# Attention with rotary embedding and a gated mixture of experts on one core: projections of q and k one step earlier, layer norm's scaling on ScalarE, weight pieces stored in order of use

## What is computed

```
x = x + tanh(g_xattn) * xattn(layernorm(x), ctx, ctx, wq, wk, wv, wo)
x = x + tanh(g_ffn) * ffn(layernorm(x), ...)

layernorm(x) = (x - mean) / sqrt(var + 1e-5)
xattn: qh, kh = rope(q @ wq.T), rope(k @ wk.T);  vh = v @ wv.T
       scores = qh . kh * 64**-0.5, masked to j <= i and j >= i - 64
       out = softmax(scores) @ vh;  return out @ wo.T
ffn:   shared = sum over 2 of gelu(x @ up.T) @ down.T
       gate = softmax(x @ router_w.T), all but the 4 largest set to 0
       routed = sum over 16 of (gelu(x @ up.T) * gate) @ down.T
```

## Time and profile before

| | |
|---|---|
| median of the runs | 569.51 us |
| the profiled execution's own time | 570.26 us |
| its span in the profile | 568.4 us |
| mean granted TensorE clock | 0.976 |
| busy: PE, DVE, ACT, POOL | 525.7, 343.6, 292.7, 274.7 us |

### The profile page before, as it was taken

One profiled execution on the slowest core, in us unless ns is written; L12 is line 12 of the kernel. 1 busy time (PEld: TensorE's weight loads), 2 busy tenths in 40 slices (PEclk: granted clock), 3 DMA queues, 4 the chain that ended last, 5 costly groups with the idle time before them and its releaser, 6 DMA issues.

```text
span 568.4 us, 13047 instructions
## 1 busy us (share of the span) xinstructions
PE 525.7 (92%) x4914; PEld 463.4 (82%) x4914; DVE 343.6 (60%) x1075; ACT 292.7 (51%) x832; POOL 274.7 (48%) x187
## 2 busy tenths in 40 slices
PE   8869789999989999899899879999999999999997
PEld 5558678889878888788887767888989898899996
DVE  5946486565965756865577553756464646554444
ACT  3275555656466555557556675554335333533332
POOL 2898886687678668767967961620010001000000
PEclk9979899999989999989999989989999999999999
DMA  7622403110031011001202227400900090036000
GB/s 241 195 51 77 107 15 95 34 35 14 23 104 36 3 34 35 10 26 35 70 3 52 73 75 248 144 1 4 329 5 1 27 309 2 1 96 240 1 1 37
DMA packets 20173, 41.02 MB, mean 72 GB/s; under 512 B 2896, under 2 KB 3152, under 8 KB 20112
## 3 DMA queue, kind: packets, MB, share of 16 engines
q1 hardware_dynamic: 20112, 40.20, 22.6%
HBM read 30.62 MB, written 2.23 MB: 58 GB/s over the span
## 4 chain that ended last, share of the span: by engine, by line
PE 72%; DVE 13%; issue 6%; ACT 3%; POOL 3%; DMA 1%; POOLq 0%; SPq 0%; DVEq 0%; ACTq 0%
PE ring L802 48%; PE psS L802 8%; PE psO L1000 5%; PE psS L969 5%; PE psT L981 4%; DVE xn L618 3%; DVE arena L638 2%; DVE arena L635 1%; ACT prob L540 1%; DVE wl L705 1%; DVE oTl L692 1%; DVE prob L684 1%; DMA x<-in_x 1%; DVE stats L607 1%; PE psT L942 1%
## 5 line engine op out<-in xcount | busy, mean ns | idle before, releaser
L802 PE MATMUL ring<-xTh,wh 128*128 128x512 f32 x272 | 110.8, 407 | 2.9 <-DVE wl L705 1.3
L802 PE MATMUL ring<-xTh,wl 128*128 128x512 f32 x272 | 106.5, 392 | 0.0
L802 PE MATMUL ring<-xTl,wh 128*128 128x512 f32 x272 | 106.0, 390 | 0.0
L484 ACT ACTIVATE sneg<-ring 128x512 f32<-128x512 f32 x72 | 43.3, 601 | 108.8 <-PE ring L802 99.3
L802 PE MATMUL ring<-wh,oTh 128*128 128x256 f32 x272 | 79.9, 294 | 7.9 <-ACT arena L526 5.7
L684 DVE TENSOR_TENSOR prob<-sneg,arena 128x512 f32<-128x512 f32 x64 | 44.1, 690 | 68.5 <-ACT sneg L484 68.5
L400 POOL TENSOR_TENSOR arena<-arena,sin 128x1024 f32<-128x1024 f32 x29 | 69.7, 2403 | 29.6 <-DVE arena L635 29.6
L413 POOL TENSOR_TENSOR prob<-prob,rinv 128x512 f32<-128x512 f32 x64 | 66.9, 1045 | 31.6 <-DVE rinv L767 30.8
L802 PE MATMUL ring<-wh,oTl 128*128 128x256 f32 x272 | 78.5, 289 | 0.0
L802 PE MATMUL ring<-wl,oTh 128*128 128x256 f32 x272 | 78.3, 288 | 0.0
L408 POOL TENSOR_TENSOR arena<-arena 128x1024 f32<-128x1024 f32 x29 | 68.9, 2377 | 1.2
(11 more groups left out here) (116 smaller groups left out, 1229.2 us busy)
## 6 DMA issues: line engine op xcount, KB each, us to landing
arena<-gate_scratch SPq DMA_DIRECT2D x64, 256.0 KB, 6.5
raw<-in_e SPq DMA_DIRECT2D x18, 256.0 KB, 2.7
raw<-in_w SPq DMA_DIRECT2D x16, 256.0 KB, 3.4
arena<-arena SPq DMA_DIRECT2D x16, 256.0 KB, 3.1
arena<-arena SPq DMA_DIRECT2D x16, 192.0 KB, 3.4
craw<-in_ctx SPq DMA_DIRECT2D x4, 512.0 KB, 3.4
x<-in_x SPq DMA_DIRECT2D x4, 512.0 KB, 4.8
out<-x SPq DMA_DIRECT2D x8, 256.0 KB, 3.1
```

The costliest lines, as they stand in the source:

```text
L484: act.activation(act_g[:, n % 2, :], ring[0][:, n % 2, :], ACT.Gelu).then_inc(f_gelu, 1)
L802: last = pe.matmul(out, a, b, start=start and i == 0 and j == 0, stop=stop and i == n - 1 and j == 2, skip_group_check=check)
```

## The change

It moves jobs in the list of steps, and each engine follows:

- q of unit u + 2 is projected in step 3 of unit u, ahead of y (before: q of unit u + 1 in step 0). k of unit u + 1 is projected in step 0 instead of step 1; in the last unit of a batch it stays in step 1. v stays in step 2. The transposes of the next batch's `xn` move from step 2 to step 1 of the third unit.
- POOL turns and joins q in step 0 and k in the steps 1 and 2 (2 and 3 in the last unit of a batch), and divides ahead of turning.
- At the start k of unit 1 leaves the prologue for step 0, and q of unit 1 enters it.
- ACT writes `xn` as `rstd * x + shift`. POOL makes `shift` = -mean * rstd with two more small operations.
- Weight pieces are numbered by `ORDER`, in order of use, and made two a step in unit 0 and one a step in unit 1. Of the experts' pieces 4 are made before the expert phase instead of 8, besides the two shared ones.

```diff
+ORDER = [("k", 0), ("v", 0), ("q", 0), ("q", 1), ("k", 1), ("v", 1), ("y", 0), ("q", 2), ("k", 2), ("v", 2),
+         ("y", 1), ("q", 3), ("k", 3), ("v", 3), ("y", 2), ("y", 3)]
+PIECE_OF = {name: i for i, name in enumerate(ORDER)}
+PRELOADED = 4
...
         prologue = [("ctx", 0), ("w", 0), ("stat", 0), ("w", 1), ("norm", 0), ("w", 2), ("k", 0),
-                    ("v", 0), ("xT", 0), ("warm", 2), ("w", 3), ("w", 4), ("q", 0), ("w", 5), ("w", 6),
-                    ("k", 1), ("warm", 3)]
+                    ("v", 0), ("xT", 0), ("warm", 2), ("w", 3), ("q", 0), ("w", 4), ("q", 1), ("warm", 3)]
...
-            if k == 0 and u + 1 < UNITS:
-                jobs.append(("q", u + 1))
-            if k == 1 and 1 <= u and u + 1 < UNITS:
+            if k == (1 if g == GROUPS - 1 else 0) and u + 1 < UNITS:
                 jobs.append(("k", u + 1))
-            if (u, k) == (0, 1) or (k == 2 and 1 <= u and u + 1 < UNITS):
+            if k == (1 if u == 0 else 2) and u + 1 < UNITS:
                 jobs.append(("v", u + 1))
-            if k == 2 and g == 2 and b + 1 < B:
+            if (g, k) == (2, 1) and nextb:
                 jobs.append(("xT", b + 1))
+            if k == 3 and u + 2 < UNITS:
+                jobs.append(("q", u + 2))
             if k == 3 and u >= 1:
                 jobs.append(("y", u - 1))
...
-            if u < 2 and k >= 2:
-                jobs += [("w", 8 + 4 * u + 2 * (k - 2)), ("w", 9 + 4 * u + 2 * (k - 2))]
+            if u == 0:
+                jobs += [("w", 5 + 2 * k), ("w", 6 + 2 * k)]
+            if u == 1 and k < 3:
+                jobs.append(("w", 13 + k))
...
-            if UNITS - 2 <= u < UNITS:
-                jobs.append(("w", expert_piece(NS + 4 * (u - (UNITS - 2)) + k)))
+            if UNITS - 2 <= u < UNITS and k % 2:
+                jobs.append(("w", expert_piece(NS + 2 * (u - (UNITS - 2)) + k // 2)))
...
+                late = int(u % GROUPS == GROUPS - 1)
+                if k == 0 and u + 1 < UNITS:
+                    if c:
+                        divide(c - 1)
+                    turn(0, u + 1)
+                    join(0, u + 1)
+                elif 1 <= c <= CHUNKS:
+                    divide(c - 1)
                 if u + 1 < UNITS:
-                    if k == 1:
-                        turn(0, u + 1)
-                        join(0, u + 1)
-                    if k == 2 and u:
+                    if k == 1 + late:
                         turn(1, u + 1)
-                    if k == 3 and u:
+                    if k == 2 + late:
                         join(1, u + 1)
...
+            def normalise(j):
+                act.wait_ge(ln_rstd, j + 1)
+                if j:
+                    act.wait_ge(xT_pe, j)
+                for t in range(TT):
+                    last = act.activation(xn[:, t, :], x[:, j % B, t, :], ACT.Identity,
+                                          bias=shift[:, t:t + 1], scale=rstd[:, t:t + 1])
+                last.then_inc(ln_norm, 1)
```

More of the change, by code:

```diff
@@ L223, in build @@
         after = {n: [] for n in range(N + 2)}
-        for e in range(NS + 8, NE):
-            after[e - 8].append(("w", expert_piece(e)))
+        for e in range(NS + PRELOADED, NE):
+            after[e - PRELOADED].append(("w", expert_piece(e)))
         for b in range(B - 1):
@@ L396, in turn @@
             def turn(i, n):
[L397 to L402, removed]
+                part = swap[:, i, :, :]
+                pool.wait_ge(qk_swap[i], rotated(n))
+                link(pool.tensor_tensor(part, part, sin[:, :].unsqueeze(1).to_broadcast(part.shape),
+                                        ALU.mult))
             def join(i, n):
                 dst = (qT[:, n % 2, :, :], kT[:, n % 2, :, W:])[i]
[L406 to L409, removed]
+                pool.wait_ge(qk_mul[i], rotated(n))
+                pool.tensor_tensor(dst, dst, swap[:, i, :, :], ALU.add).then_inc(qk_rot[i], 1)
             def divide(c):
@@ L427, in do @@
                                        ALU.subtract).then_inc(c_lo, 1)
-                elif kind in "qk" and n < 1 + (kind == "k"):
+                elif (kind, n) in (("q", 0), ("k", 0)):
                     i = "qk".index(kind)
-                    if n == 0:
+                    if kind == "k":
                         pool.wait_ge(in_rope, 32)
[L432 to L436, removed]
-                                                sin[:, :].unsqueeze(1).to_broadcast(part.shape),
-                                                ALU.mult))
-                        pool.wait_ge(qk_mul[i], done)
-                        pool.tensor_tensor(dst[:, pairs, :], dst[:, pairs, :], part,
-                                           ALU.add).then_inc(qk_rot[i], 1)
+                    for pair in range(2):
+                        part = swap[:, i, pair, :]
+                        dst = (qT, kT)[i][:, 0, pair, W * i:W * i + L]
+                        pool.wait_ge(qk_swap[i], pair + 1)
+                        link(pool.tensor_tensor(part, part, sin[:, :], ALU.mult))
+                        pool.wait_ge(qk_mul[i], pair + 1)
+                        pool.tensor_tensor(dst, dst, part, ALU.add).then_inc(qk_rot[i], 1)
                 elif kind == "stat":
@@ L611, in statistics @@
                 last.then_inc(ln_stat, 1)
-            def normalise(j):
-                dve.wait_ge(ln_rstd, j + 1)
-                if j:
-                    dve.wait_ge(xT_pe, j)
-                for t in range(TT):
-                    last = dve.tensor_scalar(xn[:, t, :], x[:, j % B, t, :], mv[:, t, 0:1],
-                                             rstd[:, t:t + 1], ALU.subtract, ALU.mult)
-                last.then_inc(ln_norm, 1)
             def rotate(job):
@@ L1064 @@
     wo = a(L0_xattn_wo).reshape(D, GROUPS, 2, P).transpose(1, 3, 2, 0).reshape(GROUPS, P, PIECE)
-    w = np.stack([wk, wv, wq, wo], 1).reshape(WPIECES, P, PIECE)
+    by_kind = dict(k=wk, v=wv, q=wq, y=wo)
+    w = np.stack([by_kind[kind][g] for kind, g in ORDER])
     up = np.concatenate([a(L0_ffn_shared_up), a(L0_ffn_routed_up)]).reshape(NE, P, KC, P)
```

37 lines of the change are left out of this document (19 added, 18 removed).

## The result

| | before | after |
|---|---|---|
| median of the runs | 569.5 us | 574.5 us |
| profiled execution: its own time, span | 570.26, 568.4 us | 574.98, 573.2 us |
| mean granted clock | 0.976 | 0.984 |
| scores of unit 2 start at | 63.85 us | 72.64 us |
| unit 2 to unit 15 | 259.6 us | 247.8 us |

The ratio is 1.0086 (95% interval 1.0063 to 1.0109): 0.9% slower, where 2.1% faster was forecast. The attention gained 11.8 us between the units 2 and 15. The start lost 8.8 and the experts 7.7, which is more.

The account below looks back on a forecast made before the run. PE, busy 92% of the span, was taken as the bound, so gains come from its idle time or slow clock. The terms summed to -12.2 us: 558.1 us profiled, 557.3 us median, ratio about 0.979, range 550 to 567.

Parts of the forecast that it names:

- start, until the scores of unit 2: Start of the kernel: q(0) comes later, POOL's chain ahead of unit 2's scores ends later, +4.0 us.
- units 2, 6, 10: Units normalising the next batch: scaling goes to ACT at 2.0 us, slow clock taken to be gone, -8.6 us.
- plain units 4, 5, 8, 9: Attention: the 0.73 us wait for the join goes, 1.44 us of waits in step 1 come, +2.8 us for four.
- units 3, 7, 11: Last units of a batch: k stays in step 1 and covers ACT's copy, 0.56 us less each, -1.7 us.
- units 12 and 13: Attention: the wait for the join goes and the wait in step 1 comes, together -0.75 us.
- unit 14: Attention: no q any more and two weight pieces fewer on POOL, 17.4 us instead of 20.87, -3.5 us.
- unit 15: Attention: two weight pieces fewer, -1 us.
- experts: First batch: DVE's 3.33 us scaling and PE's 2.06 us wait go, -3.4 us; nothing for the other two.
- the upper end: ACT's scaling of four tiles would take 4.8 us if POOL's work stretched it as it does DVE's.
- The clock didn't fall in step 1: Rival: the new waits in step 1 make the clock fall, 19 us come back, 576 us; chance 0.08.
- ACT's scaling wasn't stretched: Rival: ACT is the new bound around the scaling at 4.8 us each, 569 us; chance 0.06.
- POOL's chain at the start 5 us longer: Rival for the start: 564 us; chance 0.13, shared with half the upper price of ACT's scaling.

Follow-up runs that it names:

- run 8: The kernel before with an unused tensor of 16 bytes on a partition where the changed kernel has shift: 571.1 us, ratio 1.0037.
- Run 7: The changed kernel with the three normalisations among the experts on DVE, the others still on ACT: 569.8 us, ratio 0.9997.
- run 3: The changed kernel with the start's schedule of the kernel before, scaling still on ACT: 571.3 us, ratio 1.0051.
- run 6: The changed kernel with the start's schedule of the kernel before and the first normalisation alone on DVE: 568.8 us, ratio 0.9985.
- run 2: The changed kernel with all normalisation back on DVE and without POOL's two operations for shift: 582.8 us, ratio 1.025.
- run 11: The kernel before with 32 unused bytes on a partition where the changed kernel has shift: 571.0 us, ratio 1.0025.
- run 12: The kernel before with 16 unused bytes on a partition ahead of oTh and oTl and 48 behind them: 570.1 us, ratio 1.0009.
- run 5: The changed kernel with eight pieces of the experts' weights rounded in the attention phase in place of four: 574.4 us, ratio 1.0087.
- run 1: The changed kernel with the tensor shift laid behind all other tensors: 573.4 us, ratio 1.0081.
- run 9: The changed kernel with 48 unused bytes on a partition behind shift, so later tensors stand 64 bytes further than before: 572.7 us, ratio 1.0051.

## Why the prediction was wrong

The profiled span went from 568.4 to 573.2, +4.8 us, where -12.2 was forecast. By the prediction's own terms:

| term | forecast | profile |
|---|---|---|
| start, until the scores of unit 2 | +4.0 | +8.8 |
| units 2, 6, 10 | -8.6 | -7.5 |
| plain units 4, 5, 8, 9 | +2.8 | +2.4 |
| units 3, 7, 11 | -1.7 | -2.3 |
| units 12 and 13 | -0.75 | -1.0 |
| unit 14 | -3.5 | -3.3 |
| unit 15 | -1 | 0.0 |
| experts | -3.4 | +7.7 |

**Plain units, last units, 12 to 14: right** in mechanism and size. **Units 2, 6 and 10: right**, with ACT's scaling at 2.08 us (2.0 taken, not the 4.8 of the upper end), but 1.5 of the 1.9 us that unit 6 gained is the fall of the clock (run 8). Against the old order without one, the new unit 6 gains 0.3. The prediction took the slow clock to be gone, and it was; why the new order has it less often no run shows.

**The experts are the step that failed**, 11 of the 17 us between sum and profile. The sentence was: "ACT's scaling in its place makes the next gelu 0.9 late, of which 0.5 is hidden: -3.4 us for the first batch, nothing for the other two." It counted only the scaling's length. The gelu is behind the scaling in ACT's list, so ACT's wait for `shift` stands ahead of it as well: 2.43 + 2.08 us, and PE waits 1.88. Run 7 shows it: 1.9 us each at steps 26 and 44, and with the third the fall of the clock (which came in five of seven traces with ACT's norm there; runs 3 and 6 took 5.7 us without it). In the first batch nearly nothing was to be gained: with DVE's scaling and no fall of the clock step 8 takes 5.8 (runs 2, 7, 11 and 12), with ACT's 5.7. The start at 374.62, from which the prediction took its 3.4 us, stood behind a stretch at half clock, from 370.8 to 374.3, that the sum didn't see. "Four more pieces in this phase lie in ACT's and POOL's idle time" was right for these two engines and forgot DVE, which lost 1.1 us beside one piece and PE 1.7 (run 5). And the other steps' 2.5 us (7.7 less what stands in the table of steps and 0.3 in step 45) had no term at all: a tensor of 16 bytes a partition moved the stationary operands of the down products off a multiple of 64 bytes (runs 1, 8, 9, 11, 12).

**The start was mis-sized**, +8.8 for +4.0. The late q(0) was right to 0.1 us. Its consequence was not: the clock fell during it, and unit 0's scores came 3.1 us later. And the queue on DVE was costed by DVE's own work, without the 2.58 us wait for POOL's join of q(0), which the new order puts between q(0) and q(1). POOL is the last ahead of unit 2, as forecast, and its own work was summed rightly: from the first divide to the end of the last join (72.54, with the scores at 72.64) it has 30.3 us of work, where 30.6 was counted. But the first divide came 3.5 us later than the 35.7 taken, and the wait for piece 7 was 3.01 and not 1.4. Run 3 gives back 4.5 us of the 8.8, run 6 a further 3.9, of which some 1.6 is the fall of the clock.

**Unit 15** didn't gain its 1 us: two pieces fewer on POOL, but PE waits there for ACT's copies (0.65, 1.44 and 0.69 us).

**The rivals.** The clock didn't fall in step 1, not once in 8; in unit 15 it did, in the kernel before as well. ACT's scaling wasn't stretched. "POOL's chain at the start 5 us longer" had the right size, 4.8 us over the forecast, but the chain grew by what it waited for, DVE and ACT, not by work of POOL.

## What to carry to other kernels

Moving an operation to an idle engine also moves what it waits for: its wait blocks whatever that engine would have done next, so ask what stands behind it at each place and split the move by stage if the answers differ (here ACT in attention, DVE at the start and among the experts). Of two executions with the same code one can have a fall of the clock that the other has not, so a gain read from a unit with a slow clock is partly that fall; compare such a unit with one at full clock, and over several executions. After adding a tensor look whether those behind it moved off a multiple of 64 bytes.

## What the runs showed of the hardware

- With the stationary operands of the down products (float32r, 128x128) 16 or 32 bytes off a multiple of 64 bytes on each partition, 16 expert steps take 45.28 us for 44.48, 1.8%. Why was not tried. The starts of matmuls say which product pays: in the mean of the 16 steps the down products take 1.445 us for 1.410 and the up products, which don't read `oTh` or `oTl`, 1.385 for 1.370. So some 70% of the loss is in the down products, and how the rest gets into the others is open. One step of the kernel before, in PE's timeline (first up, first down, next up product), then one of run 12:

```profile
527.97 0.40 PE L802 MATMUL ring<-xTh,wh 128*128 128x512 f32 x1
...
529.34 0.28 PE L802 MATMUL ring<-wh,oTh 128*128 128x256 f32 x1
...
530.75 0.40 PE L802 MATMUL ring<-xTh,wh 128*128 128x512 f32 x1
```

```profile
529.43 0.40 PE L804 MATMUL ring<-xTh,wh 128*128 128x512 f32 x1
...
530.82 0.28 PE L804 MATMUL ring<-wh,oTh 128*128 128x256 f32 x1
...
532.26 0.40 PE L804 MATMUL ring<-xTh,wh 128*128 128x512 f32 x1
```

- Whether the clock falls at one place of the kernel differs between executions. In step 8 of the experts, where PE had waited 2.06 us in the kernel before and 1.88 in the changed one, it fell to half for 3.4 us in the first and not in the second; run 3 has the same wait of 1.88 and the fall. The step took 5.7 to 5.8 us in six of the profiled executions, 6.6 in one and 7.0 to 7.5 in seven, among kernels with the norm on either engine, so a fall cost some 1.5 us.
- DVE's scaling of four 128x256 tiles took 1.38 us with POOL idle, 3.33 beside POOL's weight pieces and 3.54 beside its join (run 2); ACT's took 2.06 to 2.08 in each place where it was read.
